# Fourteen places instead of eight for the gathered rows of a mixture-of-experts layer, with six gathers moved ahead of the first scatter

## The reference

```python
x = x + attention0(layernorm(x))        # 16 heads of 16, one shared k and v
x = x + ffn0(layernorm(x))              # 2 experts, top 1, 1024 wide
x = x + ssm1(layernorm(x))              # selective scan, 8 states
x = x + ffn1(layernorm(x))              # 64 experts, top 6, 2048 tokens, 176 wide, plus shared experts
```

```python
g = silu(einsum('ech,ehf->ecf', buf, w_gate))     # buf: 64 experts x 64 token rows x 256
u = einsum('ech,ehf->ecf', buf, w_up)
d = einsum('ecf,efh->ech', g * u, w_down)
y = sum over a token's 6 experts of d * its weight
y = y + (silu(x @ sh_gate.T) * (x @ sh_up.T)) @ sh_down.T   # shared experts, 352 wide
```

## Time and profile before

| what | value |
|---|---|
| median of 3 runs | 686.12 us (685.46 to 688.4) |
| the profiled execution: span | 687.0 us; no other time is listed for it |
| PE busy | 580.7 us, 85% |
| DVE busy | 513.6 us, 75% |
| ACT busy | 194.3 us, 28% |
| POOL busy | 126.6 us, 18% |
| queue q1 (SP) moved | 85.97 MB |
| queue q0 (POOL) moved | 17.21 MB |

### The profile page before, as it was taken

One profiled execution on the slowest core, in us unless ns is written; L12 is line 12 of the kernel. 1 busy time (PEld: TensorE's weight loads), 2 busy tenths in 40 slices (PEclk: granted clock), 3 DMA queues, 4 the chain that ended last, 5 costly groups with the idle time before them and its releaser, 6 DMA issues.

```text
span 687.0 us, 7110 instructions
## 1 busy us (share of the span) xinstructions
PE 580.7 (85%) x2169; PEld 328.1 (48%) x2169; DVE 513.6 (75%) x1182; ACT 194.3 (28%) x380; POOL 126.6 (18%) x121
## 2 busy tenths in 40 slices
PE   7569999689998869987899947969689899989954
PEld 6445565435555346553356423544255444434543
DVE  6989888066896849999689998589998465456535
ACT  1112221126432244331553212522201223222100
POOL 2121120300002000030000030000000466678600
PEclk9889999899999959999799986889889999999979
DMA  7941000309101191010550011994056299996488
GB/s 278 408 162 47 16 31 1 123 17 356 42 0 58 45 339 67 1 62 0 217 191 24 1 39 63 368 379 165 0 198 220 76 310 347 355 344 119 60 282 344
DMA packets 62740, 105.72 MB, mean 154 GB/s; under 512 B 6097, under 2 KB 51921, under 8 KB 62193
## 3 DMA queue, kind: packets, MB, share of 16 engines
q1 hardware_dynamic: 51792, 85.97, 35.4%
q0 software_dynamic: 8608, 17.21, 9.9%
q10 hardware_dynamic: 2304, 2.10, 0.9%
HBM read 79.80 MB, written 25.46 MB: 153 GB/s over the span
## 4 chain that ended last, share of the span: by engine, by line
PE 35%; DVE 34%; DMA 16%; issue 6%; ACT 4%; POOL 3%; SPq 1%; DVEq 0%; POOLq 0%; ACTq 0%
DMA part_rows<-bc,att_s 11%; PE gate_ps L740 7%; DVE scan_area L1370 7%; PE up_ps L740 6%; PE misc_ps L757 5%; PE turn_ps L678 4%; DVE scan_area L1366 3%; DVE scan_area L1373 3%; DMA bc<-part_rows 3%; PE ssm_ps L789 2%; PE misc_ps L851 2%; PE misc_ps L776 2%; DVE work L1462 2%; DVE sig L1310 1%; DVE keep L1460 1%
## 5 line engine op out<-in xcount | busy, mean ns | idle before, releaser
L1370 DVE TENSOR_TENSOR_SCAN scan_area<-scan_area 128x1024 f32<-128x1024 f32 x32 | 73.3, 2292 | 4.7 <-DVE scan_area L1366 0.9
L740 PE MATMUL gate_ps<-big,front_area 128*128 x144 | 74.9, 646 | 1.4 <-ACT front_area L940 1.4
L789 PE MATMUL ssm_ps<-scan_area,ident 128*128 128x512 f32 x128 | 63.3, 627 | 12.2 <-DVE scan_area L1373 11.4
L740 PE MATMUL up_ps<-big,front_area 128*128 x144 | 69.8, 607 | 0.0
L757 PE MATMUL misc_ps<-big,front_area 128*128 x288 | 65.6, 381 | 4.2 <-ACT front_area L940 3.8
L757 PEld LDWEIGHTS misc_ps<-big,front_area 128*128 128x128 f32 x288 | 54.3, 190 | 18.4 <-issue 11.8
L976 ACT ACTIVATE sig<-gate_ps 128x512 f32<-128x512 f32 (+1 forms) x48 | 28.6, 596 | 106.9 <-PE up_ps L740 65.6
L663 POOL DMA_INDIRECT part_rows<-bc,att_s x32 | 50.5, 1577 | 21.9 <-DMA part_rows<-bc,att_s 14.0
L1040 ACT ACTIVATE scan_area<-scan_area,a_col 128x511 f32<-128x511 f32 x64 | 42.2, 713 | 40.3 <-DVE scan_area L1370 36.3
L634 POOL DMA_INDIRECT front_area<-ysorted_dram,slot_idx x16 | 18.8, 1176 | 185.5 <-DMA ysorted_dram<-front_area 181.8
L699 PE MATMUL ssm_ps<-zeros,ident 128*128 128x256 f32 x112 | 32.7, 450 | 16.9 <-ACT front_area L940 13.0
(11 more groups left out here) (275 smaller groups left out, 937.8 us busy)
## 6 DMA issues: line engine op xcount, KB each, us to landing
bc<-bc_dram SPq DMA_DIRECT2D x4, 4096.0 KB, 13.6
big<-in_wgu SPq DMA_DIRECT2D x14, 704.0 KB
part_rows<-zeros SPq DMA_DIRECT2D x16, 512.0 KB, 15.3
front_area<-in_wgu SPq DMA_DIRECT2D x6, 704.0 KB
scan_area<-in_wgu SPq DMA_DIRECT2D x6, 704.0 KB
big<-part_rows SPq DMA_DIRECT2D x8, 512.0 KB, 6.4
big<-in_wd SPq DMA_DIRECT2D x12, 256.0 KB
table<-row_area SPq DMA_DIRECT2D x4, 640.0 KB, 7.9
```

What stands on the lines that cost most here:

```text
L740: mm = pe.matmul(bank[:], xs_t[:, k, j, :], gu0[:, expert_of[b, j], k, g, half * 512:(half + 1) * 512], start=(k == 0), stop=(k == K - 1))
L789: mm = pe.matmul(ssm_ps[:], ident[:], hs[:, g % HS_RING, n, :], start=False, stop=(g % PER_CHUNK == PER_CHUNK - 1 and n == GROUP - 1))
L1370: nc.vector.tensor_tensor_scan(buf.rearrange(flat), d_a[:, g % 2, :, :].rearrange(flat), buf.rearrange(flat), 0.0, ALU.mult, ALU.add).then ...
```

## The change

Six more places for gathered rows are made, three in `gate_t` and three in `sig`, both free after the shared experts of the last batch. `ROW_RING` becomes 14. The first eight gathers stay where they are, in tables.3. After the hand-written order POOL waits for `gu_used` of shared_mm.3.2, which says that both buffers are free, and issues gathers 8 to 13; in the loop it issues `fetch(p + 14)` ahead of scatter p, so the last fetch stands at pair 17 and not at pair 23. PE and DVE read from the place p % 14.

```diff
-ROW_RING = 8
+ROWS_EARLY, ROWS_IN_GATE, ROWS_IN_SIG = 8, 3, 3
+ROW_RING = ROWS_EARLY + ROWS_IN_GATE + ROWS_IN_SIG
...
-        xg = [carve(XW) for _ in range(ROW_RING)]
+        xg = [carve(XW) for _ in range(ROWS_EARLY)]
+        xg += [gate_mem[0][:, n * XW:(n + 1) * XW] for n in range(ROWS_IN_GATE)]
+        xg += [sig[:].rearrange("p s f -> p (s f)")[:, n * XW:(n + 1) * XW] for n in range(ROWS_IN_SIG)]
...
-                for p in range(ROW_RING):
+                for p in range(ROWS_EARLY):
                     fetch(p)
 
             run(pool, dict(route_slots=route_slots, ffn_out=ffn_out, gates=gates, tables=tables))
 
+            pool.wait_ge(gu_used, gu_uses_to("shared_mm", B - 1, 2))
+            for p in range(ROWS_EARLY, ROW_RING):
+                fetch(p)
             for p in range(PAIRS):
                 pool.wait_ge(yo_halves, 2 * (p + 1))
                 if p + ROW_RING < PAIRS:
```

## The result

The changed kernel takes 694.82 us (692.1 to 697.84), the kernel before, run beside it, 688.45 us (685.46 to 691.13). The ratio is 1.010, 95% interval 1.0081 to 1.012: slower by 1%, where 0.4% faster was forecast. The profiled execution has 693.91 us with a span of 692.2.

A forecast was written before the change was run, and what follows sets the result against it. Scatter landings bound the kernel up to scatter 17, then POOL's pace behind PE. Scatter 17 some 0.6 us late, then scatter 31 at PE's floor, 650.4 against 652.93: 686.12 - 2.5 = 683.6 us, range 682.0 to 686.3.

The forecast's parts named there:

- Six gathers moved ahead: Ahead of scatter 0: gathers 8 to 13 issue every 1.257 us, so scatter 0 goes out 0.42 us late.
- Slower: Rival, 544 to 558 us: POOL held at each moved gather, loop 6.3 us late, 689.9 us in all; chance 0.07.
- the full stretch: Scatter 0 to scatter 17, bound by scatter landings: keeps its bytes and its 63.03 us, no gain there.
- the wait for gu_used: POOL, ahead of the moved gathers: costs nothing, as DVE ends at 541.51 and POOL's eighth gather at 543.92.
- the fixed piece behind the last scatter: Last landing of 3.78 us, then SP's part_rows loads, 18.39 us from 664.33: unchanged, moves with the last scatter.
- a transfer of the six that delays scatter 0's landing: Near 552 us: the last one or two moved gathers meet the weights and delay scatter 0's landing by 0.2 us.
- the tail: Scatter 17 to 31, without gathers: scatters alone at 2.33 us would end at 648.8, but PE's floor of 650.4 counts.
- the floor from PE: Scatter 29 waits for weigh(29), scatter 31 for its landing, 4.46 us later: 650.4 with the delay, gain 2.5 us.
- C: Follow-up theory of PE's late reports: the ring of fourteen with its semaphores causes them.
- B: Follow-up theory of PE's late reports: the new places in gate_t and sig cause them.
- D: Follow-up theory of PE's late reports: the bytes in flight cause them, whoever moves them.
- A: Follow-up theory: a long unbroken row of gathers on GpSimd holds back what TensorE reports.

The follow-up runs named there:

- e5: Kernel before with its ring of eight, plus six unread blocks written into gate_t and sig by SyncE's plain transfers: 685.74 us.
- g2: Kernel before plus six unread blocks fetched into gate_t and sig by SyncE's plain transfers, in another session: 690.49 us.
- g3: Kernel before plus six unread blocks issued by GpSimd as plain transfers behind the row of eight gathers: 690.09 us.
- h1: Kernel before plus six unread blocks issued by GpSimd as plain transfers, once more on another chip: 686.63 us.
- i1: Changed kernel without edit, timed in a session where nothing is late: 687.79 us against 687.22, ratio 0.999.
- e1: Changed kernel again without edit: 695.64 us against 689.95.
- e2: Changed kernel, but gathers 8 to 13 are issued when yo of pair 0 is ready, behind that wait: 693.68 us.
- f1: Changed kernel again without edit, in another session: 695.03 us, ratio 1.0108.
- f2: Changed kernel with its six more places in w_sh (four), work and bc: 695.53 us, ratio 1.0115.
- e7: Changed kernel with its six more places in w_sh (four), work and bc, in another session: 687.07 us.
- g1: Changed kernel once more without edit, in another session: 684.74 us against 688.26.
- f4: Changed kernel, fourteen places, but no gathers 8 to 13 ahead of the loop; pairs 2, 4, .. 12 fetch two rows: 688.27 us, ratio 1.0013.
- e4: Changed kernel with eleven places: three more instead of six, all in gate_t: 693.59 us.

## Why the prediction was wrong

**The step that failed** is "Six gathers moved ahead": it took POOL's issue as the only price and let PE run beside it unhindered. What the runs showed in its place: where PE's reports come late, PE stands for 7.71 us beside the row, and scatter 0 comes 28.04 us after the row's start, not some 18.8. The rival "Slower" had the right place, 544 to 558 us, and too small a loss, 6.3 us against 9.6, by the wrong mechanism: the issue stays at 1.25 us, and it is PE that stands. What it got right was luck. The loss adds up. In the kernels with a ring of eight and nothing late, scatter 0 stands 18.1 us after the start of the row (e5, g2, g3, h1). In the profile after, gate_up(2) is 20.36 us after that start against 12.31 in i1, so 8.05 late; gate_up(3) follows in 5.05 us at the lowered clock, not in 3.13, another 1.92. 18.1 + 8.05 + 1.92 = 28.07, measured 28.04. Each microsecond goes to the end, as forecast, for the full stretch does not shrink.

**Right:** the wait for gu_used costs nothing (the gathers run on without a gap); the pace of issue, 1.25 us; where PE is not late, scatter 0 at 18.78 us, 0.36 behind before, forecast 0.42 (it is 0.7 behind the 18.1 of a ring of eight with nothing late; the profile before is itself of the late kind); the full stretch, 63.25 and 63.11 us against 63.03; the fixed piece behind the last scatter. Of a transfer of the six that delays scatter 0's landing nothing can be seen: scatter 17 is no later for it.

**Mis-sized:** the tail. Forecast from scatter 17 on was 650.4 - 616.2, some 34.2 us, set by the floor from PE. Over the eight traces with fourteen places and the row in one piece (after, e1, e2, f1, f2, e7, g1, i1) it is 35.3 to 36.5. In seven of them the chain goes through PE and weigh(29), as forecast. i1 shows what was too small. From weigh(19) to weigh(29) it takes 28.73 us, 28.63 before, and scatter 29 follows 1.41 us after the start of weigh(29), 1.33 in the forecast. But scatter 29 now takes 4.74 us to land, and scatter 31 starts 5.46 us behind it, where the forecast took over 4.46 from before. That is 1.0 of the 1.2 us that are missing; the restart behind the landing is 0.7 us, as forecast, and the landing is what was taken too small. In g1 and e7 the last landing that holds PE is also one pair later, that of scatter 16 and not of 15. In the profile after the scatters' own chain binds instead: scatter 17 takes 6.24 us to land, scatter 19 stands 6.97 us behind it and not 4.66, and the other twelve steps take 28.3 us, 2.36 each.

Without the hole the change is worth 1.45 us by the timelines of i1 and 1.06 by g1, where 2.5 was forecast. Both are counted against the profile before, which is of the late kind; the kernel before was never traced, with nothing added, in the other. The measured 0.999 of i1 can't tell 1.45 us from nothing, and the forecast's 0.9963 lies just outside its interval.

**What stays open** is the cause of the late reports. C falls by e2 and f4, B by f2. D was only argued against: in the changed kernel the DMA engines move 104 GB/s in the hole and 349 GB/s from 560 to 625 us with no report of PE late. f4 has the same bytes too, but not in one piece, so it does not separate D from A. A fits e1 to e4 and f1 to f4 but for the late tanh at 568.64 of e2, and whether it takes indirect gathers or any long row on GpSimd was not settled, as the plain transfers never met the kind in which reports are late. What sets the kind is open too. Each timed execution here was also recorded, so the recording itself may have held PE back; no run was made without it. The Trainium skill, "NOTIFIC — the notification-queue block", section "Overflow: three behaviours, one of which stalls the engine", says that the pipeline inside the block that writes trace records always holds its producers back rather than lose a record, and that stalls counted there would mean that it had throttled an engine. No run here shows such a count. The missing records do not show it either: by that page a record is not lost in that pipeline. Most of the missing ones are landings of transfers (3,771 to 4,002 recorded in the late kind, 4,666 to 4,781 in the other), and they are missing where PE is on time as well: from 30 to 70 us after the start of the row, in the full stretch, f1 has 520 of them and i1 809.

## What to carry to other kernels

Moving transfers into idle time of one queue is not free by the idle time alone: look at what the other engines do in the same microseconds, and leave a row of gathers no longer than the trace has shown harmless. Count a change in parts from a fixed event of its own (here the first gather), since the work ahead of it varied by 4 us and the effect is 1.5. And where a stall's releaser is "remote" and the instruction it reads had long ended, run the same kernel in another session before looking for the cause in the kernel.

## What the runs showed of the hardware

- In one kind of execution PE's semaphore updates arrive up to 8 us after the matmuls end, near the end of a row of GpSimd's gathers (in e2 also behind gathers and scatters in turn); in the other kind, with the same kernel, never (f1 and i1: 9.59 and 2.28 us from gate_up(1) to gate_up(2)).
- Even a row of eight has a trace of it: gate_up(1) follows gate_up(0) by 2.67 us in the kernel before and by 2.84 in f4, but by 2.32 or 2.33 in all ten traces of the other kind.
- After 7.71 us without work PE's next eight matmuls took 2.62 us and not 1.40, with a granted clock of 0.74 from 552 to 560 us, so a hole costs PE more than its length.
- A scatter of 128 rows lands 3.8 us after its issue as the last one of all (scatter 31 of i1), 4.74 us as scatter 29 of i1, and 6.8 to 8.5 us in the full stretch.
